# Seven or eight context tiles of each batch instead of four as three rounded products, the shift's products one place later, its seed taken straight from PSUM

## The reference, cut to what matters

```python
kv = context @ Wkv;  k, v = jnp.split(kv, 2, axis=-1);  q = x @ Wq     # 16 heads of 64
dots = jnp.einsum('bhnd,bhmd->bhnm', q, k) * SCALE
dots = dots - (1.0 - mask)[:, None, :, None] * MASK_NEG
attn = jax.nn.softmax(dots, axis=-1)                                   # over 1500 context rows
out = jnp.einsum('bhnm,bhmd->bhnd', attn, v)                           # then @ Wout + bout
x = x + xattn(layernorm(x), ctx, mask);  x = x + ffn(layernorm(x))     # ffn: gelu between w1[e] and w2[e]
```

## Time and profile before

| | before |
|---|---|
| median of 3 runs | 374.76 us |
| the profiled execution | 374.87 us |
| its span, first to last instruction | 373.0 us |
| PE busy | 363.0 us (97%) |
| DVE busy | 279.3 us (75%) |
| ACT busy | 255.1 us (68%) |
| POOL busy | 116.1 us (31%) |
| PE on the chain that ended last | 85% |
| DVE on it | 10% |

### The profile page before, as it was taken

One profiled execution on the slowest core, in us unless ns is written; L12 is line 12 of the kernel. 1 busy time (PEld: TensorE's weight loads), 2 busy tenths in 40 slices (PEclk: granted clock), 3 DMA queues, 4 the chain that ended last, 5 costly groups with the idle time before them and its releaser, 6 DMA issues.

```text
span 373.0 us, 5778 instructions
## 1 busy us (share of the span) xinstructions
PE 363.0 (97%) x1713; PEld 278.7 (75%) x1713; DVE 279.3 (75%) x458; ACT 255.1 (68%) x335; POOL 116.1 (31%) x125
## 2 busy tenths in 40 slices
PE   6899999999999999999999999999999999999996
PEld 6767777777777887777777877777777877687755
DVE  4888677978797669878797669878797669454863
ACT  3556576697769576697679476697579467796621
POOL 1610573245324430145324440255224440022000
PEclk9999999999999999999999999999999999999998
DMA  7686268329932854339932764349933752438400
GB/s 239 216 195 176 54 129 199 85 83 168 201 94 82 150 98 134 82 104 235 233 88 86 144 113 117 84 117 235 222 86 100 129 108 40 119 68 156 74 2 6
DMA packets 30622, 47.10 MB, mean 126 GB/s; under 512 B 2011, under 2 KB 21371, under 8 KB 30608
## 3 DMA queue, kind: packets, MB, share of 16 engines
q0 software_dynamic: 9936, 27.40, 37.6%
q1 hardware_dynamic: 20672, 19.52, 17.5%
HBM read 24.59 MB, written 0.23 MB: 67 GB/s over the span
## 4 chain that ended last, share of the span: by engine, by line
PE 85%; DVE 10%; issue 2%; ACT 1%; DMA 1%; SPq 0%; DVEq 0%; ACTq 0%
PE ps_s L444 29%; PE ps_a L484 23%; PE ps_x L500 10%; PE ps_a L477 9%; PE ps_x L533 3%; PE ps_a L421 2%; PE ps_x L553 2%; PE ps_x L458 1%; DVE shift_diag L930 1%; DVE ex_sum L900 1%; DMA ex_all<-in_wk_t 1%; PE ps_x L562 1%; DVE chunk_max L919 1%; DVE ex_lo L915 1%; PE ps_x L530 1%
## 5 line engine op out<-in xcount | busy, mean ns | idle before, releaser
L919 DVE TENSOR_REDUCE chunk_max<-ps_x 128x1 f32<-128x500 f32 x168 | 111.1, 677 | 31.9 <-PE ps_x L500 28.8
L708 ACT ACTIVATE ex_all<-ps_s 125x896 f32<-125x896 f32 x95 | 87.1, 917 | 44.1 <-PE ps_s L444 42.7
L484 PE MATMUL ps_a<-ex_all,ctx_sb 125*128 125x448 f32 x248 | 110.9, 541 | 0.0
L726 ACT COPY ps_s<-shift_row 125x896 f32<-125x896 f32 x94 | 85.7, 911 | 12.2 <-DVE shift_row L1057 9.7
L500 PE MATMUL ps_x<-ctxt_hi,qk_hi 128*128 128x500 f32 x168 | 80.7, 484 | 1.1 <-DVE chunk_max L919 0.9
L1234 POOL DMA_DIRECT2D ex_all<-ex_all x48 | 42.2, 878 | 115.9 <-ACT ex_all L708 111.6
L444 PE MATMUL ps_s<-qk_hi,ctxt_hi 128*125 128x448 f32 x192 | 76.3, 479 | 0.0
L484 PEld LDWEIGHTS ps_a<-ex_all,ctx_sb 125*128 125x128 f32 x248 | 46.3, 190 | 17.1 <-issue 12.7
L444 PE MATMUL ps_s<-qk_hi,ctxt_lo 128*125 128x448 f32 x192 | 54.9, 367 | 0.0
L444 PE MATMUL ps_s<-qk_lo,ctxt_hi 128*125 128x448 f32 x192 | 54.7, 366 | 0.0
L444 PEld LDWEIGHTS ps_s<-qk_hi,ctxt_hi 128*125 128x125 f32 x192 | 35.9, 187 | 24.4 <-issue 23.3
(11 more groups left out here) (110 smaller groups left out, 382.1 us busy)
## 6 DMA issues: line engine op xcount, KB each, us to landing
ex_all<-ex_all POOLq DMA_DIRECT2D x48, 448.0 KB, 4.6
ctxt_raw<-in_ctx_t SPq DMA_DIRECT2D x8, 750.0 KB, 6.5
ctx_sb<-in_ctx SPq DMA_DIRECT2D x8, 750.0 KB
ctxt_hi<-in_ctx_t POOLq DMA_DIRECT2D x21, 250.0 KB, 3.1
w_sb<-in_w SPq DMA_DIRECT2D x4, 512.0 KB, 5.0
w_sb<-in_w SPq DMA_DIRECT2D x8, 256.0 KB, 6.6
ex_all<-in_wq_t SPq DMA_DIRECT2D x2, 256.0 KB, 3.8
ex_all<-in_wk_t SPq DMA_DIRECT2D x2, 256.0 KB, 4.8
```

The lines of the kernel that those rows point to most:

```text
L484: mm = nc.tensor.matmul(ps_a[:, c, 0:CH], ctx_sb[0:MT, u, t, :], ex(t)[0:MT, c * CH:(c + 1) * CH], start=(slot == 0), stop=(slot == TM - 1))
L708: nc.scalar.activation(half(ex(t)[0:MT, :]), src, ACT.Exp, scale=SCALE).then_inc(ex_ready, 1)
L726: nc.scalar.copy(ps_s[0:MT, t % 2, :, 0:CH], half(shift_row[0:MT, b.parity, :])).then_inc(seeded, 1)
L919: nc.vector.tensor_reduce(chunk_max[:, k, t:t + 1], filled()[:, 0:MC], AX.X, ALU.max).then_inc(job_free, 1)
```

## The change

- `SPLIT` grows from tiles 2, 4, 6, 8 to 0, 2, 4, 6, 7, 8, 9, 10, and `PV_ORDER` puts tile 6 ahead of 7, 8 ahead of 9, and 11 ahead of 10. In the last batch tile 10 stays in float32, so it has seven split tiles. The context's high and low parts are made in two parts of four tiles (`CTX_PARTS`).
- ACT makes the high parts of all split tiles; that of tile 10 goes ahead of the next batch's first seed. `first_seed` copies the shift straight from `ps_x` into `ps_s`, then copies it to `shift_row` too; DVE's `shift_copies` remain for the first batch only. `shift_row` and `ex_sum` have one copy instead of two, and `sum_hi` lies in `shift_diag`'s memory. `sum_high_part` moves from step 0 to step 1, ahead of `att_out`.
- The shift's two products move from (10, 2), inside the context product, to (10, 3), behind it. The maximum at (2, 2) moves to (8, 1) before a pair batch's hidden layer, and to (4, 0) in the other batches.
- GpSimd makes the low part of the context's first four tiles in step 6 of the batch before and the second four in step 4 of the batch itself; it makes the low part of the transposed context in steps 6 and 8 instead of 2, 6 and 8.

```diff
-    SPLIT = [2, 4, 6, 8]
-    PV_ORDER = [0, 1, 2, 3, 5, 4, 7, 6, 9, 8, 10, 11]
-    SPLITS, CTX_HI_AT = len(SPLIT), 5
+    SPLIT = [0, 2, 4, 6, 7, 8, 9, 10]
+    PV_ORDER = [0, 1, 2, 3, 5, 4, 6, 7, 8, 9, 11, 10]
+    SPLITS, CTX_HI_AT = len(SPLIT), (5, 11)
+    CTX_PARTS = [slice(0, 4), slice(4, 8)]
...
-    FIRST_SHIFT_AT, SHIFT_AT = (0, 1), (TM - 2, 2)
+    FIRST_SHIFT_AT, SHIFT_AT = (0, 1), (TM - 2, 3)
 
-    ADD_AT = {(10, 2): (0,), (11, 0): (1, 2)}
-    ADD_LATE = (3, 4)
+    ADD_AT = {(10, 2): (0,), (11, 1): (1, 2)}
+    ADD_LATE = {(0, 0): (3, 4)}
+    LOW_AT = [(t + 1, 1) for t in SPLIT[:-1]] + [(11, 0)]
...
+        def buffer_free(n):
+
+            return read_by(SPLIT[n - 2]) if n >= 2 else read_by(SPLIT[SPLITS - 2 + n]) - TM
...
                         for c in range(2):
                             mm = nc.tensor.matmul(ps_a[:, c, 0:CH], a[0:MT, u, n, :], e[0:MT, n % 2, c * CH:(c + 1) * CH],
-                                                  start=False, stop=False)
+                                                  start=(slot == 0 and term == 0), stop=(slot == TM - 1 and term == 2))
...
+            def first_seed(b):
+
+                act.wait_ge(job_ready, jobs.value())
+                act.wait_ge(ex_ready, b.at(TM, -1))
+                nc.scalar.copy(ps_s[0:MT, 0, :, 0:CH], ps_x[0:MT, :, 0:CH]).then_inc(seeded, 1)
+                nc.scalar.copy(half(shift_row[:, :]), ps_x[:, :, 0:CH]).then_inc(job_free, 2)
...
                     exponentials(b, t)
                     if t == 1 and b.off > 0:
+                        sum_high_part(b.later(-1))
                         att_out(b.later(-1))
+                    if prepare and t == TM - 2:
+                        ex_high_part(b, SPLITS - 1)
...
-                        seed(b.later(1), t + 2 - TM)
-                    if t == 0 and b.off > 0:
-                        sum_high_part(b.later(-1))
...
                     if prepare and at == SHIFT_AT:
-                        shift_copies(b.later(1))
+                        jobs.n += 2
...
-                        ctxt_lo_chunk(b.later(1), 0)
+                    if t == 4:
+
+                        pool.wait_ge(ex_lo_ready, b.at(SPLITS, 2))
+                        ctx_low_part(b, 1)
                     if prepare and t == 6:
 
-                        pool.wait_ge(ex_lo_ready, b.at(SPLITS, 2))
-                        ctxt_lo_chunk(b.later(1), 1)
-                        ctx_low_part(b.later(1))
+                        pool.wait_ge(ex_lo_ready, b.at(SPLITS, 3))
+                        for k in range(2):
+                            ctxt_lo_chunk(b.later(1), k)
+                        ctx_low_part(b.later(1), 0)
                     if prepare and t == 8:
 
-                        pool.wait_ge(ex_lo_ready, b.at(SPLITS, 3))
+                        pool.wait_ge(ex_lo_ready, b.at(SPLITS, 4))
                         ctxt_lo_chunk(b.later(1), 2)
```

More of the change, by code:

```diff
@@ L566, in shift_jobs @@
             def shift_jobs():
-                for c in range(2):
+                for _ in range(2):
+                    c = jobs.n % 2
                     shift_rows(job()[:, 0:CH], P, c, start=True).then_inc(job_ready, 1)
@@ L849, in _ @@
             for h in range(HEADS):
+                if h == HEADS - BEHIND:
+                    for part in range(2):
+                        ctx_high_part(Batch(None, 0), part)
                 drain_later_queries(h)
@@ L1109, in add @@
                 def add(at):
[L1110 to L1112 removed]
+                    for n in ADD_LATE.get(at, ()) if b.off > 0 else ():
+                        add_to_sum(b.later(-1), n)
                     for n in (ADD_AT if prepare else LAST_ADD_AT).get(at, ()):
                         add_to_sum(b, n)
[L1115 to L1116 removed]
+                    if at in LOW_AT and (prepare or LOW_AT.index(at) < SPLITS - 1):
+                        ex_low_part(b, LOW_AT.index(at))
                 for t in range(TM):
```

80 lines of the change are left out of this document (41 added, 39 removed), and 6 rows, old and new, of the table MAX_AT.

## The result

The changed kernel takes 376.39 us (median of 20 runs, 375.85 to 377.80) against 374.90 us for the kernel before (20 runs): ratio 1.0037, interval 1.0023 to 1.0050. It is 1.5 us slower. That lies in the predicted range and in the forecast's "within 1%", but not on its side: 374.5 us was forecast, 0.3 us faster.

What follows compares the result with a forecast made beforehand. PE, busy 363.0 of 373.0 us, was taken as the bound; 8.4 us saved there and the waits added elsewhere summed to -0.3 us, from 374.87 to 374.6, forecast 374.5 us by median, range 367.5 to 379.5.

Steps and rivals of the forecast that it cites:

- H: Last batch, without maxima: 0.8 us of PE's gain lost behind ACT, tile 9's low part 0.2 us; 1.0 us together.
- C: Output job waits for ACT's second copy from the shift's bank, 0.2 to 0.3 us late; 0.7 us for three.
- PE's gain: Each tile changed from float32 to split saves PE 0.27 us; 31 tiles, 8.4 us gained.
- A: Shift in a pair batch: tile 7's low part lengthens DVE's chain, PE's wait 1.32 us instead of 0.51; 2.4 us.
- B: Hidden layer: its bank waits for the reduction of the maximum put ahead, 0.3 us three times; 0.9 us.
- D: Shift in the other batches: PE comes 0.5 us later, so the handover wait vanishes four times; 0.6 us gained.
- E: DVE's backlog in step 1: PE stands 0.4 us in four batches, 0.1 us in two; 1.8 us.
- F: Logarithm in step 3 late, maxima of step 4 wait: 0.25 us in four batches, 0.1 in two; 1.2 us.
- G: First batch: tile 0's low part goes among four back-to-back reductions, 1.0 us less 0.3 of slack; 0.7 us.
- Rival 1: Most waits along the kernel are absorbed: E to H vanish, C in half; 369.4 us, chance 0.27.
- Rival 2: ACT's `att` comes late at every batch's seam, stopping PE: 5.6 us on top, 380 us, chance 0.20.
- Rival 3: The four-pass rule's larger gain per float32 product, on top of the forecast's waits: 371.3 us, chance 0.03.

Runs made afterwards that it cites:

- last_batch_four: Changed kernel with tiles 7, 8 and 9 in float32 in the last batch alone (four split tiles there instead of seven): 375.39 us, ratio 1.0007.
- six_tiles: Changed kernel with tiles 0, 2, 4, 6, 7, 8 split, tile 7's low part ahead of the hidden layer, four split tiles in the last batch: 374.50 us.
- five_tiles: As six_tiles, with tile 0 in float32 too (2, 4, 6, 7, 8 split; 2, 4, 6 in the last batch): 373.66 us, ratio 0.9968.

## Why the prediction was wrong

It said -0.3 us and it was +1.5. The step that failed is **H, the last batch**.

- **H** was priced at 1.0 us and cost 2.7: the last stretch grew by 1.59, where five split tiles should give 1.35 and the last output job's wait (C) cost 0.23. That is 1.7 us of the 1.8 that are missing. H had two parts, PE's gain in tiles 7 to 9 (0.8 us, lost) and tile 9's low part at 0.2 of its 1.0 us. The first was right. The second failed: PE already waited 0.27 us for DVE's list there, so there was nothing to hide it, and last_batch_four gives 1.10 us for leaving tiles 7 to 9 away, on top of PE's 0.8. The last 0.8 us are at the head of the batch, where the prediction put nothing: PE stood 0.32 us at the attention's output (below), and by the starts 0.53 us at its first context product. That product waits for ACT's `att`, though the profile names no releaser:

```profile
323.64 0.91 ACT L749 COPY att<-ps_a 128x896 f32<-128x896 f32 x1
324.77 0.64 PE L486 MATMUL ps_a<-ex_hi,ctx_hi 125*128 125x448 f32 x2 [0.37 <-issue]
```

  ACT runs without a pause from 319.28 to the end of `att` at 324.55, with tile 0's high part and the sum's in it, and PE has no maxima in this batch that would hold it back. In the kernel before, `att` ended at 324.33 and the product started at 324.47, less than 0.1 us late.
- **PE's gain** of 0.27 a tile held: 0.29 for tile 0, from six_tiles against five_tiles in steps 2 and 3.
- **A** was right in size: waits of 1.35 us against the 1.32 forecast, the chain 7.39 against 7.46. But it was a term that could not be had back alone: behind it lay ACT's list of the same length, which the prediction never laid beside PE for steps 9 to 11 except for C.
- **B** 0.37 (0.3 forecast), **C** 0.23 (0.2 to 0.3), **D** no handover wait (185.59 follows its product): right.
- **E** was too large, 0.08 us at each turn instead of 0.4: the chain on DVE took 7.7 us (8.0 forecast), and PE was there later than I had it. **F** was too small, 0.43 in four batches and 0.17 in two instead of 0.25 and 0.1. Together they were about 2.5 us for 3.0, and B was 0.2 more than forecast; by these the rounds should have come out near -0.4, and the rest to the measured -0.23 is not assigned. That the rounds met their forecast is partly luck, since E's error and F's cancelled.
- **G** 0.95 us for 0.7, most of the first batch's +0.3: PE stood at a maximum in step 2 of the first batch, behind the subtraction.
- **Rivals.** Rival 1 did not happen: E shrank, but C stayed whole and B, F, G and H grew. Rival 2 did not happen in the rounds: no context product there was released by ACT's `att`. At the head of the last batch it did, once, for the 0.5 us above. Rival 3's four passes would have given 0.37 a tile against the 0.29 seen.

Most waits stood where they were put. The batch which has no maxima was judged by averages ("its 0.8 us of PE's gain are lost", "0.2 us") and not by laying DVE's and ACT's lists out as was done for A.

## What to carry to other kernels

Lay out the last iteration by itself, instruction by instruction: it has no work after it that hides anything, so a saving on the bound engine can be void there and an addition to the list that feeds the final product can count in full. Where two engines' lists of nearly the same length run side by side, shortening one gave nothing here; move the common head of both earlier, or take work out of both. And split only so many tiles as the helpers can feed: without tile 10 a round was 0.54 us shorter than with it, and one maximum's better place gave 0.67 more.
